# A conv-and-experts kernel on Trainium2: the work ahead of its first product written anew

## What is computed

```python
def involution(x):                        # of the normalised x
    patches = conv_general_dilated_patches(x, (7, 7), (1, 1), [(3, 3), (3, 3)])
    h = einsum('bchw,oc->bohw', x, reduce_w) + reduce_b        # 128 -> 32
    kern = einsum('bchw,oc->bohw', h, span_w) + span_b         # 32 -> 49 * 16
    return (kern * patches).sum(axis=taps)

x = x + involution(layernorm_over_channels(x))
t = tokens(x)                             # 12544 x 128
n = layernorm(t)
gates = top 2 of softmax(n @ router_w.T), scaled to sum 1
t = t + sum over the two experts of gate * ((silu(n @ w1.T) * (n @ w3.T)) @ w2.T)
```

## Time and profile before

| | |
|---|---|
| timed runs, us | 1468.66 median of 3 (1464.93 to 1470.01) |
| the profiled execution, us | 1463.2, its span 1461.4 |
| mean granted TensorE clock | 0.971 of full speed |
| TensorE busy | 1286.7 us, 88% |
| VectorE busy | 1072.8 us, 73% |
| POOL busy | 831.7 us, 57% |
| ScalarE busy | 416.7 us, 29% |

### The profile page before, as it was taken

One profiled execution on the slowest core, in us unless ns is written; L12 is line 12 of the kernel. 1 busy time (PEld: TensorE's weight loads), 2 busy tenths in 40 slices (PEclk: granted clock), 3 DMA queues, 4 the chain that ended last, 5 costly groups with the idle time before them and its releaser, 6 DMA issues. The chain is left out here.

```text
span 1461.4 us, 25064 instructions
## 1 busy us (share of the span) xinstructions
PE 1286.7 (88%) x8596; PEld 1126.6 (77%) x8596; DVE 1072.8 (73%) x2250; ACT 416.7 (29%) x1055; POOL 831.7 (57%) x573
## 2 busy tenths in 40 slices
PE   0598888999999999999999999999999999985973
PEld 0387777788888888888888888887888888874862
DVE  2599998887887878878788887888878878641320
ACT  2112020331433324333142331423323232252431
POOL 1233544457566575765756657566574755755655
PEclk9999998999999999999999999999999999997996
DMA  5001010333334333342343433433324243356763
GB/s 151 13 0 39 18 48 17 107 73 98 84 73 119 70 97 83 73 116 64 89 101 73 100 79 90 101 71 87 91 70 112 60 103 68 90 137 149 170 150 44
DMA packets 91230, 123.38 MB, mean 84 GB/s; under 512 B 13042, under 2 KB 68466, under 8 KB 91104
## 3 DMA queue, kind: packets, MB, share of 16 engines
q1 hardware_dynamic: 54592, 94.96, 21.4%
q0 software_dynamic: 36512, 26.83, 12.8%
HBM read 87.18 MB, written 34.56 MB: 83 GB/s over the span
## 5 line engine op out<-in xcount | busy, mean ns | idle before, releaser
L878 DVE TENSOR_TENSOR prod<-kern_ps,xn 128x896 f32<-128x896 f32 x686 | 733.7, 1084 | 75.6 <-PE kern_ps L480 69.4
L402 PE MATMUL acc_ps<-consts_sb,prod 128*128 128x128 f32 x3920 | 544.9, 275 | 0.0
L480 PE MATMUL kern_ps<-h_stack,span 98*128 98x448 f32 x1372 | 478.0, 432 | 70.0 <-DVE prod L878 67.7
L1016 POOL DMA_INDIRECT out<-y_sb,xs x210 | 330.8, 1575 | 318.7 <-ACT y_sb L656 236.0
L402 PEld LDWEIGHTS acc_ps<-consts_sb,prod 128*128 128x128 f32 x3920 | 470.9, 142 | 52.3 <-issue 12.2
L1025 POOL TENSOR_TENSOR prod<-prod 128x896 f32<-128x896 f32 x126 | 270.7, 2148 | 146.8 <-DVE prod L878 144.3
L480 PEld LDWEIGHTS kern_ps<-h_stack,span 98*128 98x128 f32 x1372 | 228.7, 194 | 114.9 <-DVE prod L878 97.3
L996 POOL DMA_INDIRECT sorted_x<-rows,dst x196 | 190.7, 973 | 71.2 <-issue 56.3
L643 ACT ACTIVATE silu<-hid_ps 114x256 f32<-114x256 f32 x228 | 87.6, 384 | 417.7 <-PE hid_ps L504 417.5
L898 DVE TENSOR_TENSOR hid<-hid_ps,silu 114x256 f32<-114x256 f32 x228 | 96.0, 421 | 99.5 <-ACT silu L643 98.3
L503 PE MATMUL hid_ps<-xc,w_sb 128*114 128x256 f32 x456 | 136.6, 381 | 1.3
(11 more groups left out here) (96 smaller groups left out, 936.4 us busy)
## 6 DMA issues: line engine op xcount, KB each, us to landing
w_sb<-in_w SPq DMA_DIRECT2D x105, 342.0 KB, 3.4
w_sb<-in_w SPq DMA_DIRECT2D x105, 192.0 KB, 3.0
xs<-sorted_x SPq DMA_DIRECT2D x105, 130.0 KB, 2.2
x_ln<-in_x SPq DMA_DIRECT2D x14, 448.0 KB, 3.5
x_res<-in_x SPq DMA_DIRECT2D x14, 448.0 KB, 3.4
out<-x_res SPq DMA_DIRECT2D x14, 448.0 KB, 3.1
out<-y_sb,xs POOLq DMA_INDIRECT x210
sorted_x<-rows,dst POOLq DMA_INDIRECT x196, 2.3
```

The source lines that it names most:

```text
L402: return mm(dst, lhsT=src, rhs=eye, is_transpose=True, start=start, stop=True, skip_group_check=True)
L480: i = mm(kern_ps[:, n % 2, h, 0:HALF], span[:, u * C:(u + 1) * C], h_stack[:, m % 2, h * HALF:(h + 1) * HALF], start=True, stop=True)
L878: v.tensor_tensor(tiled(prod[:, n % PRING, :].rearrange("p (h n) -> p h n", h=2)), tiled(kern_ps[:, n % 2, :, 0:HALF]), window(m, u // KS, ...
L1016: g.indirect_dma_start(out[:, :], bass.IndirectOffsetOnAxis(ap=xs[:, j % XBUFS, b, C:C + 1].bitcast(U32), axis=0), y_sb[:, j % YBUFS, b, : ...
```

## The change

The negative slots go; each engine has a straight piece of program ahead of the loop in their place, and the loop starts at n = 0 (TensorE makes `kern(0)` ahead of it).

- *Loads.* SP's queue keeps input tile 0, consts, input tile 1, the pieces, the residual tiles. Reduction weights, bias, router, tokens and pads go to ScalarE's queue. `s_const` counts three loads (consts, weights, bias), and a new semaphore `s_late` the last three; whoever needs those waits for them at the first use (TensorE at tile 0's logits, VectorE at its token numbers, SP at the store of the pads). VectorE starts with the statistics of tile 0 and makes its casts behind them.
- *Banks.* The head's transposes and reductions write to places of `kern_ps` and `acc_ps` that are free then, with their own semaphore `s_first`; `reduce`, `channels_of_x`, `high_part` and `low_part` get place and semaphore as arguments. Loads of input tiles 2 and 3 wait on `s_first`.
- *Pieces.* They are loaded into places 2 to 8 of `prod`. ScalarE makes the high parts of pieces 0 and 1 between tile 0's evictions, the others behind tile 1's. VectorE makes the low parts of pieces 0 to 2 ahead of the first product and those of 3 to 6 ahead of products 2, 4, 6 and 8. `kern` waits at each seventh tap of tile 0 for its piece, and a product that overwrites a piece for that piece's low part.
- *Table.* ScalarE computes seven elements of `minus_half` into a new tile `warm` ahead of its first normalisation.

```diff
-            sp.dma_start(red_sb[:], w_red).then_inc(s_const, 16)
-            sp.dma_start(bred_sb[:], b_red).then_inc(s_const, 16)
             load_ln(1)
-            for i in range(7):
-                sp.dma_start(prod[0:KROWS, i, :], w_span[:, i * N:(i + 1) * N]).then_inc(s_piece[i], 16)
-            sp.dma_start(router_sb[:], router).then_inc(s_const, 16)
-            sp.dma_start(tok_sb[:], tok).then_inc(s_const, 16)
-            sp.dma_start(pads_sb[:], pads).then_inc(s_const, 16)
+            for i in range(PIECES):
+                sp.dma_start(staged(i)[0:KROWS], w_span[:, i * N:(i + 1) * N]).then_inc(s_piece[i], 16)
             load_res(0)
             load_res(1)
-            sp.wait_ge(s_const, 16 * NCONST)
+            sp.wait_ge(s_late, 16 * 3)
...
+                if m == 0 and u % (TAPS // PIECES) == 0:
+                    pe.wait_ge(s_piece_lo, u // (TAPS // PIECES) + 1)
...
-            pe.wait_ge(s_const, 16 * NCONST)
+            pe.wait_ge(s_const, 16 * 3)
+            for h in range(2):
+                channels_of_x(0, h, kern_ps[:, 0, h], s_first)
+            pe.wait_ge(s_setp, 3)
+            for h in range(2):
+                reduce(0, h, kern_ps[:, 1, h], s_first)
+            for h in range(2):
+                channels_of_x(1, h, acc_ps[:, h], s_first)
             pe.wait_ge(s_setv, 4)
-            for n in range(-2 * TAPS, SLOTS):
+            kern(0)
+            for n in range(0, SLOTS):
...
-            act.wait_ge(s_const, 16 * NCONST)
+            act.dma_start(red_sb[:], w_red).then_inc(s_const, 16)
+            act.dma_start(bred_sb[:], b_red).then_inc(s_const, 16)
+            act.dma_start(router_sb[:], router).then_inc(s_late, 16)
+            act.dma_start(tok_sb[:], tok).then_inc(s_late, 16)
+            act.dma_start(pads_sb[:], pads).then_inc(s_late, 16)
             act.wait_ge(s_setp, 3)
-            for n in range(-2 * TAPS, SLOTS):
+            act_f(warm[:], minus_half[:], ACT.Identity)
+            for k in range(3):
+                norm_x(0, k)
+            for h in range(2):
+                piece_high(h)
+                act.wait_ge(s_first, 1 + h)
+                channels_of_x(0, h, kern_ps[:, 0, h])
+            for k in range(3):
+                norm_x(1, k)
+            act.wait_ge(s_const, 16 * 3)
+            for h in range(2):
+                act.wait_ge(s_first, 3 + h)
+                high_part(0, h, kern_ps[:, 1, h])
+            for h in range(2):
+                act.wait_ge(s_first, 5 + h)
+                channels_of_x(1, h, acc_ps[:, h])
+            for i in range(2, PIECES):
+                piece_high(i)
...
+            for m in range(2):
+                dve.wait_ge(s_x_ln[m], 16)
+                ln("ln1", m, 0, lambda b: x_ln[:, m, b * C:(b + 1) * C], None)
+                ln("ln1", m, 1, None, None)
+                ln("ln1", m, 2, None, LN_C_EPS)
+                if m == 0:
+                    dve.wait_ge(s_const, 16 * 3)
+                    v.tensor_copy(upper[:], upper_f).then_inc(s_setv, 1)
+                    v.tensor_copy(ones[:], ones_f)
+                    v.tensor_copy(offset[:], region8_c).then_inc(s_setv, 1)
+                ln("ln1", m, 3, None, None)
+            for i in range(2):
+                piece_low(i)
+            for h in range(2):
+                low_part(0, h, kern_ps[:, 1, h])
+            for i in range(2, LOW_FIRST):
+                piece_low(i)
...
+                if low_of(n) is not None:
+                    piece_low(low_of(n))
+                product(n)
```

More of the change, by code:

```diff
@@ L131, in bank_uses @@
     uses = []
-    for n in range(-2 * TAPS, SLOTS + TAPS):
+    for n in range(0, SLOTS + TAPS):
         m, u = divmod(n, TAPS)
@@ L185, in build @@
         minus_half = sb("minus_half", [P, NB])
+        warm = sb("warm", [P, NB])
         xn = sb("xn", [P, XROWS * PW])
@@ L288, in build, with staged, low_of @@
         s_enough = sem("s_enough")
-        NCONST = 6
+        PIECES, LOW_FIRST = 7, 3
+        def staged(i):
+            return prod[:, PRING - PIECES + i, :]
+        def low_of(n):
+            i = LOW_FIRST + n // 2 - 1
+            return i if n % 2 == 0 and LOW_FIRST <= i < PIECES else None
         def parity_count(tile):
@@ L428, in take_bank, with reduce, channels_of_x @@
                         pe.wait_ge(s_yout, r + 1)
-            def reduce(m, h):
-                take_bank(f"red_{h}", m)
+            def reduce(m, h, dst, ready):
                 pe.wait_ge(s_xn, 2 * (m + 1))
-                mm(bank[0:3 * RED, 0:HALF], red_sb[:], half_window(m, h), start=True, stop=True).then_inc(s_bank, 1)
-            def channels_of_x(m, h):
-                take_bank(f"xn_{h}", m)
+                mm(dst[0:3 * RED, 0:HALF], red_sb[:], half_window(m, h), start=True, stop=True).then_inc(ready, 1)
+            def channels_of_x(m, h, dst, ready):
                 pe.wait_ge(s_norm["ln1"], m + 1)
@@ L691, in _ @@
                     exponentials(m - 1)
-                if n == -TAPS - 1:
-                    for i in range(7):
-                        act.wait_ge(s_piece[i], 16)
-                        act_f(span[:, i * N:(i + 1) * N], prod[0:KROWS, i, :], ACT.Copy).then_inc(s_piece_hi, 1)
             last = TILES - 1
@@ L754, in router_step @@
                     dve.wait_ge(s_bank, READY["logits", m])
+                elif k == 12 and m == 0:
+                    dve.wait_ge(s_late, 16 * 3)
                 elif k == 12 and m >= 2:
@@ L934, in _ @@
                         ln("ln1", r, 3, None, None)
-                if 0 <= m + 1 < TILES:
+                if m + 1 < TILES:
                     if u == 39:
-                        low_part(m + 1, 0)
+                        low_part(m + 1, 0, bank[:])
                     if u == 44:
-                        low_part(m + 1, 1)
-                if n == -TAPS - 1:
-                    for i in range(7):
-                        dve.wait_ge(s_piece_hi, i + 1)
-                        hi = span[64:97, i * N:(i + 1) * N]
-                        v.tensor_tensor(hi, prod[64:97, i, :], hi.bitcast(F32), ALU.subtract).then_inc(s_piece_lo, 1)
+                        low_part(m + 1, 1, bank[:])
             last = TILES - 1
@@ L1019, in _ @@
             SENDS = (29, 30, 32, 33, 36, 37, 39, 40, 41, 43, 44, 46, 47, 48)
-            for n in range(-2 * TAPS, SLOTS):
+            for m in range(2):
+                rsqrt("ln1", m)
+            for n in range(0, SLOTS):
                 m, u = divmod(n, TAPS)
-                if 0 <= m and u % 4 == 2 and (u - 2) // 4 in PAIRED:
+                if u % 4 == 2 and (u - 2) // 4 in PAIRED:
                     a = prod[:, (n - 2) % PRING, :]
```

88 lines of the change are left out of this document (50 added, 38 removed).

## The result

The changed kernel takes 1431.28 us (median of 4 runs, 1428.72 to 1435.62) against 1466.8 (1463.46 to 1470.01) for the kernel before, run beside it: a ratio of 0.9761, 95% interval 0.9726 to 0.9797. In a later batch it took 1431.97 (6 runs) against 1466.4 (11 runs), 0.9774 (0.9751 to 0.9798). The forecast was 1437.5 with a range of 1428 to 1450: right in sign, inside the range, 6 us too long.

What follows compares the result with a forecast made beforehand. The prediction took the kernel to be a chain without a clock ending in a full TensorE: 34.0 us saved in the head less 2.8 given back is 31.2 off 1468.66, so 1437.5 us, range 1428 to 1450.

Steps and rivals of the forecast that it cites:

- What bounds the kernel: Whole span: TensorE busy 88%, loop without a clock, so time saved ahead of the first product comes off one for one.
- The start: Head: VectorE waits for the first input alone, 4.04 us instead of 18.86; casts move beside POOL's power, table load leaves the path.
- the 0.4 of the loads: Head: loads on ScalarE's queue delay the first input by 0.4 us, between bounds of 0 and 0.9.
- the first rival: Head: POOL isn't ready for its power, at most 15 us lost; this or another late start 1446 to 1452 us, chance 0.12.
- Tile 0 to the first product: Head, from tile 0's normalising to the first product: stepped to 23.3 us, 23.7 with the loads' delay, against 57.72.
- The low part of piece 2 is what is late next: Head, on VectorE: this 1.02 us step ends at 23.2 and releases the first product, while TensorE's taps end at 21.7.
- Give-back: First ten products: four low parts, 4.3 us, moved between them cost 2.8 us, at least 1.8 and at most 4.3.
- stepped: First ten products stepped through at TensorE's early durations: the tenth ends at 15.3 instead of 13.0, 2.3 us given back.
- the second rival: First tile's slots: TensorE stays at its lower level, 1.0 us more per slot, a whole tile 1486 us; chance 0.03.
- The sum: Whole kernel: 34.0 us earlier first product less 2.8 given back, 31.2 us off.

Runs made afterwards that it cites:

- Experiment 1: The kernel before with router, tokens and pads on a semaphore of their own, waited for at first use: 1453.01 us against 1466.87, ratio 0.990.
- experiment 5: The changed kernel with all loads on SP's queue, none on ScalarE's: first statistic 4.55 us against 4.56, first product 22.17; no timed ratio given.
- experiment 6: Three kernels from the changed one: low parts of pieces 2 to 6 later; idle matmuls in the head; both together. Product 10 lead of the second 31.98 us.
- the last kernel of experiment 7: The changed kernel with POOL casting the high parts of pieces 2 to 6, VectorE's low parts left in place: ratio 0.9757, median 1429.34 us.
- the first kernel of experiment 7: The changed kernel with POOL casting high parts of pieces 2 to 6, only low parts 5 and 6 between products: ratio 0.9761.
- the first kernel of experiment 6: The changed kernel with pieces 2 to 6 staged in idle tiles, low parts ahead of products 12, 17, 24, 31, 39: first product 20.36 us.

## Why the prediction came out as it did

- **What bounds the kernel** was right: a chain without a clock, whose later end moves with it. Experiment 1 shows it by the runs, the lead that stays level from product 10 to 49 by the trace, the hole that moved with the loop too.
- **The start.** First statistic 4.56 (forecast 4.44), power 6.98 (6.9), normalisation 8.78, reduction 14.90 (14.5 plus the 0.4 of the loads). The 0.4 of the loads had about the right size (the first input landed 0.5 later than before); its cause, the second queue, isn't shown, as experiment 5 has the same delay with one queue.
- **POOL, the first rival**, fell: the power begins 0.16 us after its input is done, 3.75 after the last memset. The 6 us of the Trainium skill (GPSIMD Engine Reference, "2.1 Instruction dispatch") for a freshly loaded routine don't show in these rows.
- **Tile 0 to the first product: mis-sized by 1.2 us** (22.51, forecast 23.7). I priced the reduction as twice a row of two matmuls and tile 1's transposes as twice a row of four, each row with a start and an end of its own, and let the transposes wait for the reduction's end. Four reduction matmuls in a row took 3.27, not 3.6, eight transposes 1.97, not 2.4, and the transposes began 0.2 before the reduction's last matmul ended: together 1.0 of the 1.2. It is the same lower level of TensorE: single matmuls took as long as before (nanoseconds, minimum/median/maximum; the kernel before, the changed one, and the last line from experiment 6 behind the idle work).

```profile
L433 PE MATMUL bank<-xn,red_sb x4: 954/1006/1061, 50.0 to 54.0; 128*96 128x448 f32 x4
L402 PE MATMUL bank<-consts_sb,x_ln x16: 364/421/472, 27.7 to 48.9; 128*128 128x128 f32 x12, 64*128 64x64 f32 x4
...
L441 PE MATMUL kern_ps<-xn,red_sb x4: 954/954/1032, 14.9 to 17.2; 128*96 128x448 f32 x4
L411 PE MATMUL acc_ps<-consts_sb,x_ln x8: 362/420/472, 18.0 to 19.5; 128*128 128x128 f32 x6, 64*128 64x64 f32 x2
...
L441 PE MATMUL kern_ps<-xn,red_sb x4: 546/546/597, 16.2 to 17.4; 128*96 128x448 f32 x4
```

- **The low part of piece 2 is what is late next**: right; TensorE's first tap matmuls were done before it, and where the last kernel of experiment 7 ends it 1.8 us earlier, the first product comes 1.8 us earlier too.
- **Give-back**: 2.46 us, forecast 2.8, stepped 2.3. I took more than the stepped value, which was nearer.
- **The lower level, the second rival**: the taps from the third on ran at it (23.66: 2.11 us for two pairs), and it ended near 30, some 10 us after the first tap, as before. The ten products give no sign that it cost more than before.
- **The sum.** At product 10 the gain is 32.75, forecast 31.2: 1.2 of the first product and 0.3 of the give-back. The rest, up to 35.5 by the medians, isn't the head's: the stretches of lower clock fell otherwise against this trace, -1.8 us up to product 685 and +3.5 behind it. That the forecast was 6.2 us too long has a third part: the kernel before, 1468.66 when I forecast, took 1466.8 beside the changed one, 1.9 less. The intervals of both sets of runs (the second 0.9774, some 33 us) hold the 32.75.

Taken singly, the parts are worth 13.25 (the semaphore, in the kernel before), 5.65 (banks), 1.32 (table) and 1.3 (the four low parts, net). The remaining 11 or so, by difference, I lay to the order: tile 1 prepared beside tile 0, five high parts behind both, the casts beside POOL. That isn't shown: the remainder wasn't tried alone, and parts need not add up.

## What to carry to other kernels

Look at what the first instruction of each engine waits for: one semaphore counted over loads of early and late use cost 13 of these 35 us, and a few moved waits got them back. In a kernel without a clock a head's saving can reach the end in full, as here, so it is measured at the first slots of the loop; work that is moved into the loop is paid nearly whole where TensorE is full, and to some 60% where its engine waits anyway. When the profile lays a wait to a transfer, compare it with the time at which the transfer's semaphore was last raised before blaming a neighbour that runs in step with it: in the first kernel of experiment 7 the wait was the transfer's, and what the neighbour did was lengthen the instructions that it met.

## What the runs showed of the hardware

- The granted-clock column reads 1.00 from 10 to 14 us, yet eight transposes took 2.00 us there and 1.18 behind the idle work: in this sparse head the durations tell TensorE's level (1.2 or 2.4 GHz), the column doesn't (it reads 0.53 from 23 to 30 us).
- The level falls again: in the changed kernel the tap pair took 0.61 at 19.65 and 1.05 at 23.66, after 2.78 us of idling; in the first kernel of experiment 6 it fell by 22.50 after idle times of only 0.84 and 0.33. What decides it stays open.
- A low part takes 1.09 us alone and up to 1.82 beside a cast. POOL's cast of 98x896 takes 0.93 us alone and up to 1.8 beside a low part, its sum of two products 2.10 alone and 2.99 beside one (24.68 in the changed kernel).
